# The input of later groups of a convolution, attention and mixture-of-experts block: gathered by index by GpSimd in pieces instead of loaded by two direct transfers a group

## The reference

```python
x = x + conv(group_norm(x))       # two 1x1 projections (info, mask), their outer product, a third projection
t = to_tokens(x)                  # (32, 1024, 64)
t = t + attention(layer_norm(t))  # linear attention, 8 heads, then a hidden layer of 128 and two layer norms
t = t + ffn(layer_norm(t))        # 8 experts of 64 -> 128 -> 64 with gelu; each token weighs its two best
return from_tokens(t, x)

def ffn(x):                       # cut
    cw = zeros((N, E)).at[arange(N)[:, None], top2_idx].add(top2_vals)
    for e in range(E):
        out += cw[:, e, None] * (gelu(x @ W1[e] + b1[e]) @ W2[e] + b2[e])
```

## Time and profile before

| | |
|---|---|
| median of 2 runs | 1175.74 us (1174.54 to 1176.95) |
| the profiled execution | span 1171.7 us |
| granted TensorE clock, mean | 0.985 of full speed |
| TensorE busy | 1058.5 us, 90% of the span |
| VectorE, ScalarE, GpSimd busy | 740.2, 641.8 and 361.7 us |
| data moved by DMA | 88.62 MB |

### The profile page before, as it was taken

One profiled execution on the slowest core, in us unless ns is written; L12 is line 12 of the kernel. 1 busy time (PEld: TensorE's weight loads), 2 busy tenths in 40 slices (PEclk: granted clock), 3 DMA queues, 4 the chain that ended last, 5 costly groups with the idle time before them and its releaser, 6 DMA issues.

```text
span 1171.7 us, 16823 instructions
## 1 busy us (share of the span) xinstructions
PE 1058.5 (90%) x6646; PEld 442.3 (38%) x6646; DVE 740.2 (63%) x1529; ACT 641.8 (55%) x866; POOL 361.7 (31%) x280
## 2 busy tenths in 40 slices
PE   4798589979999899988999899998999989998898
PEld 1453244323533245332453235432453324532232
DVE  5744745686647875587664966468764886556344
ACT  3345355654566556664556546556556555665454
POOL 0000031333323333333232333133332342324465
PEclk9989889999999999999999999999999999999999
DMA  5000086007700284005810068000850039200760
GB/s 157 6 1 1 1 179 149 3 22 173 169 1 19 54 189 104 1 19 112 185 50 1 19 149 198 1 19 19 194 134 1 18 69 201 42 1 19 179 145 23
DMA packets 15597, 88.62 MB, mean 76 GB/s; under 512 B 3488, under 2 KB 6816, under 8 KB 11424
## 3 DMA queue, kind: packets, MB, share of 16 engines
q1 hardware_dynamic: 15520, 87.57, 32.3%
HBM read 78.12 MB, written 9.44 MB: 75 GB/s over the span
## 4 chain that ended last, share of the span: by engine, by line
PE 74%; DVE 12%; ACT 9%; issue 3%; DMA 1%; DVEq 0%; POOL 0%; POOLq 0%; SPq 0%
PE HP L847 15%; PE HP L861 14%; ACT H L992 5%; PE R L646 5%; PE R L621 4%; PE R L610 4%; PE R L699 3%; PE R L717 2%; PE R L708 2%; PE R L786 2%; PE R L795 2%; PE R L788 2%; PE R L861 2%; PE R L675 2%; DVE TM L1355 2%
## 5 line engine op out<-in xcount | busy, mean ns | idle before, releaser
L1044 POOL TENSOR_TENSOR XB<-TM,XB 128x512 f32<-128x512 f32 x254 | 323.0, 1286 | 658.5 <-DVE TM L1355 658.5
L992 ACT ACTIVATE H<-HP,W 128x1024 f32<-128x1024 f32 x224 | 243.0, 1116 | 205.7 <-PE HP L847 205.1
L1355 DVE SCALAR_TENSOR_TENSOR TM<-HP,B2S,CWB 128x512 f32<-128x512 f32 x224 | 163.2, 742 | 207.1 <-PE HP L861 196.3
L847 PE MATMUL HP<-XF,W1E 64*128 64x512 f32 x1024 | 269.9, 630 | 19.3 <-DVE TM L1355 18.5
L861 PE MATMUL HP<-H,W 128*64 128x512 f32 x896 | 233.1, 616 | 18.0 <-ACT H L992 18.0
L847 PEld LDWEIGHTS HP<-XF,W1E 64*128 64x128 f32 x1024 | 84.1, 187 | 143.9 <-DVE TM L1355 71.0
L861 PEld LDWEIGHTS HP<-H,W 128*64 128x64 f32 x896 | 48.5, 135 | 171.2 <-ACT H L992 116.3
L1156 DVE SCALAR_TENSOR_TENSOR BIG<-R,T 128x512 f32<-128x512 f32 x112 | 69.5, 681 | 20.9 <-PE R L610 20.8
L930 ACT ACTIVATE T<-R 128x512 f32<-128x512 f32 x96 | 57.4, 598 | 39.8 <-PE R L646 31.4
L958 ACT ACTIVATE T<-R,MINUS 128x512 f32<-128x512 f32 x64 | 41.4, 688 | 27.3 <-PE R L708 24.4
L1243 DVE SCALAR_TENSOR_TENSOR BIG<-T,R 128x512 f32<-128x512 f32 x64 | 41.8, 684 | 21.6 <-ACT T L958 21.6
(11 more groups left out here) (179 smaller groups left out, 1411.3 us busy)
## 6 DMA issues: line engine op xcount, KB each, us to landing
CWB<-gates_hbm SPq DMA_DIRECT2D x32, 1536.0 KB, 20.4
CWB<-gates_hbm SPq DMA_DIRECT2D x32, 512.0 KB, 6.6
out<-XB SPq DMA_DIRECT2D x15, 512.0 KB, 3.0
X<-x SPq DMA_DIRECT2D x14, 512.0 KB, 3.8
XF<-x SPq DMA_DIRECT2D x2, 512.0 KB, 6.1
gates_hbm<-RT SPq DMA_DIRECT2D x16, 64.0 KB, 1.6
W<-wpack SPq DMA_DIRECT2D x1, 968.0 KB, 4.9
W1E<-w1e SPq DMA_DIRECT2D x1, 512.0 KB, 7.4
```

The lines of the kernel that those rows point to most:

```text
L847: last = mm(HP[u % BATCH][:, half(k)], W1E[img(k), e, :], XF[img(k), 1 - par, s, half(c)], start=True, stop=True)
L992: f(activated(b, u).rearrange("p k t -> p (k t)"), HP[u % BATCH][:, :], ACT.Gelu, bias=col(B1E + e))\
L1044: nc.gpsimd.tensor_tensor(acc, TM[:, u % BATCH, :], acc, ALU.add).then_inc(acc_done, 1)
L1355: v.scalar_tensor_tensor(out=TM[:, u % BATCH, :], in0=sums_of(b, u), scalar=B2S[:, e % 2, e // 2:e // 2 + 1], in1=CWB[:, s, e, half(c)], o ...
```

## The change

SP no longer loads the inputs of groups 2 to 7. GpSimd gathers them: x is seen as rows of 64 floats (256 bytes), and a gather takes 128 of them, one for each partition, by the indices in a column of ROWS, into 64 columns of X. Sixteen pieces make a slot, 32 a group. They are issued in GpSimd's own queue during the first half of group b's units and bring group b + 2: three pieces after the add of each of units 3 to 12, and the last two after that of unit 13, for b from 0 to 5. ROWS is filled once, at the start, by an iota. The statistics of a later group wait for all 16 pieces of a slot (rows_in).

```diff
--- before.py
+++ after.py
@@ -109,6 +109,10 @@
 AHEAD = [name.partition(" ")[2] for name in OPENING if name.startswith("next ")]
 ROUTER = ("gates", "gate_tokens", "gate_exp", "choose_1", "choose_2", "gate_rows", "weights_1")
 FIRST, SECOND = "H", "Y"
+ROW = 64
+PIECE_ROWS = T // ROW
+GATHER_FROM = 3
+GATHERED_A_UNIT = 3
 BATCH = 2
 PE_STEPS, ACT_STEPS, DVE_STEPS = 1, 2, 3
 
@@ -158,6 +162,7 @@
         SPREAD = sb("SPREAD", [P, 2, P])
         GWZ = sb("GWZ", [P, 3 * 2 * E])
         GB = sb("GB", [P, 1])
+        ROWS = sb("ROWS", [P, G * PIECE_ROWS], I32)
         SM = sb("SM", [P, 4, G, NORMS])
         SG = sb("SG", [P, 4, G, 1])
         H = sb("H", [P, 2, 2, CH])
@@ -247,6 +252,8 @@
         prep_pe = sem("prep_pe")
         prep_done = sem("prep_done")
         x_in = sems("x_in")
+        rows_set = sem("rows_set")
+        rows_in = sems("rows_in")
         early_in = sems("early_in")
         gn_part = sem("gn_part")
         gn_stat = sem("gn_stat")
@@ -507,13 +514,6 @@
                 sp.dma_start(SWAP[img(r), :], wpack[img(k), swaps:swaps + P]).then_inc(swap_in, 16)
 
             def parts(a, b, par):
-                def next_input(slots):
-                    if a == 0 or a == GROUPS - 1:
-                        return
-                    for s in slots:
-                        sp.wait_ge(xs_done[s], a if a == EARLY else a + 1)
-                        sp.dma_start(X[:, s, :], xd[a * G + G + s]).then_inc(x_in[s], 16)
-
                 def gate_weights():
 
                     sp.wait_ge(cwt_done, a + 1)
@@ -549,7 +549,7 @@
                     sp.wait_ge(acc_done, b * US + (s + 1) * CH_UNITS)
                     sp.dma_start(od[b * G + s], XB[:, 1 - par, s, :]).then_inc(out_done[s], 16)
 
-                return {**slotwise("features_1", next_input), "gate_rows": gate_weights,
+                return {"gate_rows": gate_weights,
                         "weights_1": last_weights, "finish_0": lambda: store(0), "finish_1": lambda: store(1)}, lambda step, u: None
 
             turns(parts, DVE_STEPS, apart=1)
@@ -1017,6 +1017,9 @@
             nc.gpsimd.memset(KS[:, :, :, :, :], 0.0)
             nc.gpsimd.memset(SPREAD[:, :, :], 0.0).then_inc(pads_set, 1)
             nc.gpsimd.memset(MINUS[:, :], -1.0).then_inc(one_set, 1)
+            nc.gpsimd.iota(ROWS[:, :], [[P * PIECE_ROWS, G], [1, PIECE_ROWS]], base=0, channel_multiplier=PIECE_ROWS).then_inc(rows_set, 1)
+            pool.wait_ge(rows_set, 1)
+            x_rows = x.rearrange("n c (j t) -> (n c j) t", t=ROW)
             line = 2 * (NQ - 1)
             nc.gpsimd.memset(LINES[:, :], 0.0).then_inc(lines_set, 1)
             for k in range(2):
@@ -1043,9 +1046,23 @@
                     acc = XB[:, 1 - par, s, half(c)]
                     nc.gpsimd.tensor_tensor(acc, TM[:, u % BATCH, :], acc, ALU.add).then_inc(acc_done, 1)
 
+                def gather_input(piece):
+
+                    s, j = piece // PIECE_ROWS, piece % PIECE_ROWS
+                    if j == 0:
+                        pool.wait_ge(xs_done[s], b + 1 if b + 1 == EARLY else b + 2)
+                    n = s * PIECE_ROWS + j
+                    nc.gpsimd.indirect_dma_start(out=X[:, s, ROW * j:ROW * j + ROW], out_offset=None, in_=x_rows,
+                                                 in_offset=bass.IndirectOffsetOnAxis(ap=ROWS[:, n:n + 1], axis=0),
+                                                 element_offset=(b + 2) * G * P * T)\
+                        .then_inc(rows_in[s], 16)
+
                 def expert(step, u):
                     if step == SECOND:
                         add_up(u)
+                        if b + 2 < GROUPS and u >= GATHER_FROM:
+                            for piece in range(G * PIECE_ROWS)[GATHERED_A_UNIT * (u - GATHER_FROM):][:GATHERED_A_UNIT]:
+                                gather_input(piece)
 
                 return slotwise("features_1", residual), expert
 
@@ -1108,7 +1125,10 @@
                         if a == EARLY:
                             dve.wait_ge(early_in[s], 16)
                         else:
-                            dve.wait_ge(x_in[s], max(a, 1) * 16)
+                            if starting(a):
+                                dve.wait_ge(x_in[s], 16)
+                            else:
+                                dve.wait_ge(rows_in[s], 16 * PIECE_ROWS * (a - 1))
                         for c in range(NCH):
                             ins = v.bn_stats(ST[:, s, 6 * c:6 * c + 6], Xa[:, s, half(c)])
                         ins.then_inc(gn_part, 1)
```

## The result

The changed kernel takes 1209.68 us (1208.54 to 1210.83), the kernel before 1175.74 us (1174.54 to 1176.95): a ratio of 1.028, with a 95% interval of 1.023 to 1.033. It is slower by 33.9 us, 5.7 us for each of the six groups that are gathered. The forecast was 1205 us.

What follows compares the result with a forecast made beforehand. TensorE was taken to set the pace, in lockstep with ScalarE and VectorE. Late combine and landing, 3.8 us, plus port, 1.0, made 4.8 us a group, 29 us over 6 groups: 1205 us, range 1173 to 1290.

Steps and rivals of the forecast that it cites:

- What goes is worth nothing: Removing SP's 12 direct transfers of X gains 0; far end 8.25 us once, in the opening.
- The length of a turn: The pipeline's turns were taken as equal, 140.6 us each, from unit 5's add to its next on GpSimd.
- 4 to 5 us above 140.6: Sign to look for: spacing of turns this much longer in the six gathering groups, 140.6 us where nothing is gathered.
- The time of one gather, 1.29 us: Time of each gather on GpSimd, taken from its common instruction of 1.29 us; ends 0.34 and 2.34 us.
- the 1.06 us from which adds are late: Gather time up to which unit 13's add is in time for unit 15's combine at 371.4.
- hidden: Rival: a gather takes less than 1.06 us, no combine is late, 1176 us, up to 1182; chance 0.22.
- The combine of 15: VectorE's combine of unit 15 waits for GpSimd's add of unit 13: 3.4 us late, 3.1 us a group stay.
- GpSimd's backlog from the add of unit 8 on: From 347.95, six adds and 15 gathers stand before the end of unit 13's add, at 374.8 us.
- Landing, 0.7 us: Statistics of slot 1 wait 0.7 us a group for the last gather, landing 3.8 us from its issue.
- The shared port, 1.0 us: Gathers hold up small VectorE instructions: 1.0 us a group, between 0 and 3.9 us.
- The operations named: VectorE's two instructions at 317.15 and the one of 332.92, each of which could lose up to one gather.
- The sum, 4.8 us a group: 3.8 us for late combine and landing plus 1.0 for the port; over 6 groups 29 us.

Runs made afterwards that it cites:

- rows1024: Changed kernel with rows of 1024 floats, 2 gathers a group, both behind unit 3's add: 1174.3 us, ratio 1.001 to the kernel before.
- clean16: Changed kernel with 16 gathers a group of 128 floats, placed clear of the 32-wide strip matmuls: 1178.3 us, ratio 1.003 to the kernel before.
- dirty16: The same 16 gathers of 128 floats a group as clean16, placed over the strip matmuls: 1208.8 us, ratio 1.028 to the kernel before.
- idle_slots: Changed kernel with the same 192 gathers moved to where GpSimd is idle, so that no add is late: 1207.7 us, ratio 1.029.
- late_only: As idle_slots, but the last six gathers of a group all behind unit 12's add: 1241.8 us, ratio 1.057 to the kernel before.
- direct_dose: Changed kernel with each gather cut into two or three plain transfers without index list, same places: 1198.7 us, ratio 1.020.

## Why the prediction was right, and where not

The time was right within 5 us, and so were the sign and the place of the first wait. The mechanism of the late combine is as forecast; the closeness of the total is in part luck, because a large part of the loss was not in the sum.

- *What goes is worth nothing*: right. rows1024, which takes the same transfers from SP, stands at the time of before, and the opening gave nothing (the combine of unit 0 waits 8.2 us for the gate weights in both kernels).
- *The length of a turn*: the 140.6 us that the prediction took for every turn is only the first one; the steady turns of before are 138.2 us, by the residual adds. No term of the sum hangs on it, but the sign "4 to 5 us above 140.6" has to be read from 138.2.
- *The time of one gather, 1.29 us*: right, it is 1.25 us (0.95 and a pause of 0.30). The number came from the likeness to GpSimd's add, and no run shows that the two have anything in common: the pause was not foreseen. It takes the gather over the 1.06 us from which adds are late. The Trainium skill (DMA: Bandwidth & Descriptors, Latency and other measured facts) gives about 1 us to the first byte: the busy part alone would agree, but taken for the whole cost it would have led to "hidden".
- *The combine of 15*: the mechanism is as forecast, down to GpSimd's backlog from the add of unit 8 on. The term was too large: 1.88 us in five groups instead of 3.1 in six. VectorE came to that combine later itself by then (the long pair at 366.85 and the held completions), so the lateness of the add cost less.
- *Landing, 0.7 us*: wrong, it is 0. The last gather starts at 380.62 and the statistics of slot 1 some 1.2 us behind 382.29, unhindered, so the piece landed within 2.9 us, where I had taken the 3.8 us of a transfer of 512 KB.
- *The shared port, 1.0 us*: right in size for a wrong place. The operations named hardly changed; what grew is the L1251 pair, by 1.4 us in each of the six groups, because an add that the gathers had displaced came to lie beside it:

```profile
L1251 DVE SCALAR_TENSOR_TENSOR XB<-T,W,XB 128x512 f32<-128x512 f32 x32 | 31.1, 1011 | 0.0
```

against, before,

```profile
L1231 DVE SCALAR_TENSOR_TENSOR XB<-T,W,XB 128x512 f32<-128x512 f32 x32 | 23.5, 772 | 0.0
```

  It is GpSimd's add that holds VectorE; where a gather and such a pair met, the gather grew instead (1.23 us at 369.25, 1.48 at most).
- *The sum, 4.8 us a group*: 5.7 measured. The unforeseen part is the held completions, small ones of 0.4 to 1.2 us here: 8.3 us more waiting on L675 (VectorE's T and XF together), 1.8 on the denominator, 2.5 on the variance over the span. With it goes the lower granted clock, 13.4 us more of busy TensorE. These waits overlap and do not add up to the loss; the last group shows 3.7 us at the full clock; the one that ends at 747.64, at the full clock too, 5.3, with one small operation of VectorE stretched to 1.93 us (650.03); the others contain slower stretches. That the low clock follows from the stalls is likely, since clean16 has TensorE busy for 1058.3 us and dirty16 for 1070.2, but no run of the changed kernel took the stalls away and left the rest.

A forecast with only the terms that exist would have been nearer to 3.3 us a group for adds and port. The total came out because two terms that were too large (combine and landing) stood in for one that was missing, and that is luck. The lesson of idle_slots is that the mechanism which I had right, late adds, could be removed without gaining a microsecond, since the longer strings that removed it held the completions longer.

## What to carry to other kernels

A gather by index costs its issuing engine by the instruction, not by the byte: make rows as long as the layout allows, and there may be nothing left to hide. Where many must be issued, their place matters more than the idle time of GpSimd: look at which matmuls another engine is waiting for, and keep strings of gathers clear of them. And when a predicted wait shows up in the trace, remove it alone before calling it the cause.

## What the runs showed of the hardware

- Under strings of gathers with an index list the completions of TensorE's matmuls came late to VectorE and ScalarE: by 0.4 to 1.2 us under strings of three (the changed kernel), by 1.8 to 4.4 us in the longest waits of idle_slots, and by up to 6.0 us in late_only. Seen are the 32-wide strips (L662, L675, L742), the 64-wide ones of L754 and, in late_only, the first layer of an expert (L846, tiles of 64 by 128). Plain transfers issued by GpSimd, up to 444 of them, did not do it. The path by which this happens is open. The Trainium skill (SBUF — State Buffer, Who interferes with whom) says that TensorE and ScalarE never wait on anyone; that sentence stands among those on SBUF ports, and whether a port plays a part here no run shows, but a reader who takes it as a rule for scheduling would miss the 30 us between clean16 and dirty16.
- 128 rows by index: 0.95 us of GpSimd for 256 B, 512 B and 4 KB a row, then 0.30 us until the next. A plain transfer of 128 rows issued by GpSimd takes 0.54 us; all pauses between the 444 of direct_dose make 5.4 us.
- The issue of plain transfers by GpSimd stretched VectorE operations with two SBUF inputs (0.29 to 1.36 us at 374.63 in direct_dose). The Trainium skill (SBUF — State Buffer, Who interferes with whom) infers that building a transfer's entries needs the write side of the shared port pair and a tensor_tensor takes only its read side, so that the two leave each other alone; the measurement decides, and here they met.
